# Row stages of a two-layer graph attention kernel: normalizing one tile per step, a third query buffer, transposed denominators, and last rows stored by tile

## The reference

```python
def _layernorm(x, axis=-1, eps=1e-5):
    m = jnp.mean(x, axis=axis, keepdims=True)
    v = jnp.var(x, axis=axis, keepdims=True)
    return (x - m) / jnp.sqrt(v + eps)
# layer 0
x_l = (x @ W + b).reshape(N, NHEADS, C)
scores = alpha_l[:, None, :] * alpha_r[None, :, :]      # alpha: x_l times att_l, att_r
att = softmax(where(adj[:, :, None] > 0, scores, NEG_INF), axis=1)
out = relu(einsum('ijh,jhc->ihc', att, x_l))
x = _layernorm(x + out)
# layer 1: queries are x, keys x2, values v, given as inputs
scores = where(adj > 0, einsum('hnd,hmd->hnm', q * C**-0.5, k), NEG_FILL)
x = _layernorm(x + einsum('hnm,hmd->hnd', softmax(scores), vv))
```

## Time and profile before

| | us |
|---|---|
| median of three runs | 3744.48 |
| the profiled execution, whole | 3745.04 |
| its span in the trace | 3743.1 |
| first row stage, from its first load to the first load of the next stage | 1674.07 to 1825.42 |
| second row stage, from the first load to the end of the span | 3640.46 to 3743.1 |
| TensorE busy over the span | 3551.1 (95%) |
| VectorE busy over the span | 2909.1 (78%) |
| ScalarE busy over the span | 2525.6 (67%) |

### The profile page before, as it was taken

The page is one execution under the profiler, slowest core; times in us unless marked ns, Lnnn a source line. Parts: engine busy times, 40 slices in busy tenths (PEclk is TensorE's granted clock), DMA queues, the critical chain, the costliest instruction groups (busy, mean ns, idle before and its releaser), DMA issues. The chain is left out here.

```text
span 3743.1 us, 58557 instructions
## 1 busy us (share of the span) xinstructions
PE 3551.1 (95%) x22661; PEld 1448.4 (39%) x22661; DVE 2909.1 (78%) x2948; ACT 2525.6 (67%) x2430; POOL 1569.5 (42%) x1157
## 2 busy tenths in 40 slices
PE   6888899999999999987699999999999999999987
PEld 4665222222222222225344444444444444444434
DVE  5555899999999999977577777777777777777768
ACT  3444899999999999963466666666666666666642
POOL 3333010010010101011267666767666677667661
PEclk9999899999999999995699999999999999999995
DMA  7887677677777776667699999999999999999987
GB/s 259 298 299 245 153 161 165 152 160 156 162 160 161 154 160 153 153 157 254 174 198 198 205 205 201 208 197 199 204 205 200 205 201 198 205 202 203 191 188 247
DMA packets 375357, 729.43 MB, mean 195 GB/s; under 512 B 31376, under 2 KB 219792, under 8 KB 358720
## 3 DMA queue, kind: packets, MB, share of 16 engines
q0 software_dynamic: 99504, 419.90, 57.7%
q1 hardware_dynamic: 241552, 272.26, 23.8%
q10 hardware_dynamic: 34048, 33.82, 2.7%
HBM read 263.54 MB, written 59.69 MB: 86 GB/s over the span
## 5 line engine op out<-in xcount | busy, mean ns | idle before, releaser
L1130 DVE TENSOR_TENSOR a_weights<-a_psS,maskT 128x1024 f32<-128x1024 f32 x1024 | 1205.5, 1219 | 463.5 <-ACT a_psS L1095 463.5
L1095 ACT ACTIVATE a_psS<-a_psS,a_shift 128x1024 f32<-128x1024 f32 x1024 | 1071.4, 1084 | 678.8 <-PE a_psS L1023 678.7
L538 DVE TENSOR_TENSOR g_weights<-g_weights,maskT 128x1024 f32<-128x1024 f32 x1024 | 1169.7, 1218 | 117.5 <-ACT g_weights L525 117.5
L525 ACT ACTIVATE g_weights<-al_bc,g_shift,g_xl 128x1024 f32<-128x1024 f32 x1024 | 1167.9, 1228 | 88.4 <-PE g_psD L563 88.4
L1023 PE MATMUL a_psS<-a_q,a_k 128*64 128x512 f16 x8192 | 971.6, 380 | 17.0 <-DMA a_k<-k_scratch 15.5
L1040 PE MATMUL a_psO<-a_weights,a_v 128*64 128x512 f32 x4096 | 961.2, 592 | 0.0
L554 PE MATMUL g_psO<-g_weights,g_xl 128*64 128x512 f32 x4096 | 924.1, 598 | 23.2 <-DVE g_weights L538 23.2
L1153 POOL TENSOR_TENSOR a_pool_total<-a_pool_total,a_weights 128x1024 f32<-128x1024 f32 x336 | 924.3, 2751 | 0.0
L1023 PEld LDWEIGHTS a_psS<-a_q,a_k 128*64 128x64 f16 x8192 | 463.4, 110 | 647.0 <-issue 300.4
L1161 POOL DMA_DIRECT2D a_dma_total<-a_weights x480 | 467.1, 973 | 399.6 <-DVE a_weights L1130 202.5
L554 PEld LDWEIGHTS g_psO<-g_weights,g_xl 128*64 128x64 f32 x4096 | 277.9, 137 | 660.5 <-issue 530.8
(11 more groups left out here) (121 smaller groups left out, 1451.0 us busy)
## 6 DMA issues: line engine op xcount, KB each, us to landing
a_dma_total<-a_weights POOLq DMA_DIRECT2D x512, 512.0 KB, 5.4
g_total<-g_weights POOLq DMA_DIRECT2D x128, 1024.0 KB, 7.7
adj_sb<-in_adj_dram SPq DMA_DIRECT2D x128, 512.0 KB, 5.9
g_xl<-xl_scratch SPq DMA_DIRECT2D x128, 260.0 KB, 6.7
a_k<-k_scratch SPq DMA_DIRECT2D x256, 128.0 KB, 5.4
a_v<-in_L_gnn_v_dram SPq DMA_DIRECT2D x128, 256.0 KB, 3.9
al_bc<-alpha_scratch SPq DMA_DIRECT2D x16, 1024.0 KB, 6.7
f_oT<-o_scratch SPq DMA_DIRECT2D x16, 1024.0 KB, 6.8
```

The source lines that it names most:

```text
L525: nc.scalar.activation(w[:, u % RING, h, :], al_bc[:, g % 2, h, :], ACT.Exp, bias=shift_bc[:, g % 2, h:h + 1], scale=xl[:, slot, u % KB, 2 ...
L538: nc.vector.tensor_tensor(w[:, u % RING, h, :], w[:, u % RING, h, :], maskT[:, j, (g // PAIRS) * IC:(g // PAIRS + 1) * IC], ALU.mult).then ...
L1095: nc.scalar.activation(psS[n % RING][:], psS[n % RING][:], ACT.Exp, bias=shift_bc[:, g % 2, h:h + 1], scale=SCALE).then_inc(exped, 1)
L1130: nc.vector.tensor_tensor(w[:, u % NP, h, :], psS[n % RING][:].rearrange("p a c -> p (a c)"), maskT[:, j, (g // PAIRS) * IC:(g // PAIRS + ...
```

## The change

- ScalarE normalizes tile t - 4 in step t, one tile per step, where it normalized four tiles in every fourth step. A group's store of 1 MB is issued behind its fourth tile, three steps later than before. The second row stage gets 36 steps where it had 33.
- The last group of either row stage is stored as four DMAs of 256 KB, each behind its own tile, where it was one of 1 MB.
- `qh` and `ql` have three buffers of a pair (QB = 3) where they had two, with three semaphores.
- The denominators are turned by a transpose (`is_transpose=True`) into `psR`, where they were a float32 matmul by the identity.

```diff
--- before.py
+++ after.py
@@ -624,6 +624,7 @@
         R = NT // T
         ZB = 3
         LAG = 7
+        QB = 3
         PARTS = (0, 32, 64)
         K = PARTS[-1] + H
         oT = sb("oT", [P, 2, PAIRS, T * P], F32)
@@ -665,8 +666,8 @@
         res_ready = sem("res_ready")
         res_stored = [sem(f"res_stored{i}") for i in range(ZB)]
         if first:
-            qh = sb("qh", [P, 2, PAIRS, 2 * P], F16)
-            ql = sb("ql", [P, 2, PAIRS, 2 * P], F16)
+            qh = sb("qh", [P, QB, PAIRS, 2 * P], F16)
+            ql = sb("ql", [P, QB, PAIRS, 2 * P], F16)
             v_sum = sb("v_sum", [P, F], F32)
             headmask = sb("headmask", [H, F], F32)
             next_sum = sb("next_sum", [H, F], F32)
@@ -675,11 +676,11 @@
             qh_ready = sem("qh_ready")
             ql_ready = sem("ql_ready")
             v_loaded = sem("v_loaded")
-            q_stored = [sem(f"q_stored{i}") for i in range(2)]
+            q_stored = [sem(f"q_stored{i}") for i in range(QB)]
             tail = sem("tail")
 
         block = ctx.enter_context(nc.Block())
-        STEPS = NT + LAG if first else NT + 1
+        STEPS = NT + LAG if first else NT + T
 
         @block.sync
         def _(sp):
@@ -724,9 +725,10 @@
                                  skip_group_check=True)
                 if t >= 2:
                     pe.wait_ge(inverted, t - 1)
-                nc.tensor.matmul(psR[t % 2][:], dT[0:H, par, cols], identF[0:H, 0:H], start=True, stop=False)
-                nc.tensor.matmul(psR[t % 2][:], alone[:, par, cols], times_n[:], start=False, stop=True
-                                 ).then_inc(turned, 1)
+                nc.tensor.matmul(psR[t % 2][:], dT[0:H, par, cols], identF[0:H, 0:H], is_transpose=True, start=True,
+                                 stop=False, skip_group_check=True)
+                nc.tensor.matmul(psR[t % 2][:], alone[:, par, cols], times_n[:], start=False, stop=True,
+                                 skip_group_check=True).then_inc(turned, 1)
 
             def turn_queries(t):
                 r, s = divmod(t, T)
@@ -756,35 +758,40 @@
                     act.wait_ge(rstd_ready, r - 1)
                 nc.scalar.activation(std[:, r % 2, :], mv[:, r % 2, :, 1], ACT.Sqrt, bias=eps[:]).then_inc(std_ready, 1)
 
-            def normalize(r):
-                act.wait_ge(rstd_ready, r + 1)
-                act.wait_ge(offset_ready, r + 1)
-                for s in range(T):
-                    nc.scalar.activation(z[:, r % ZB, s, :], z[:, r % ZB, s, :], ACT.Identity,
-                                         bias=offset[:, r % 2, s:s + 1], scale=rstd[:, r % 2, s:s + 1]
-                                         ).then_inc(res_ready, 1)
-                act.wait_ge(res_ready, T * (r + 1))
-                act.dma_start(result[r * T * P:(r + 1) * T * P, :].rearrange("(t p) c -> p t c", p=P),
-                              z[:, r % ZB, :, :]).then_inc(res_stored[r % ZB], 16)
+            def normalize(t):
+                r, s = divmod(t, T)
+                if s == 0:
+                    act.wait_ge(rstd_ready, r + 1)
+                    act.wait_ge(offset_ready, r + 1)
+                nc.scalar.activation(z[:, r % ZB, s, :], z[:, r % ZB, s, :], ACT.Identity,
+                                     bias=offset[:, r % 2, s:s + 1], scale=rstd[:, r % 2, s:s + 1]
+                                     ).then_inc(res_ready, 1)
+                if r == R - 1:
+                    act.wait_ge(res_ready, t + 1)
+                    act.dma_start(result[t * P:(t + 1) * P, :], z[:, r % ZB, s, :]).then_inc(res_stored[r % ZB], 16)
+                elif s == T - 1:
+                    act.wait_ge(res_ready, t + 1)
+                    act.dma_start(result[r * T * P:(r + 1) * T * P, :].rearrange("(t p) c -> p t c", p=P),
+                                  z[:, r % ZB, :, :]).then_inc(res_stored[r % ZB], 16)
 
             def upper(t):
                 pair, half = divmod(t, 2)
                 act.wait_ge(q_turned, t + 1)
-                if half == 0 and pair >= 2:
-                    act.wait_ge(q_stored[pair % 2], 32 * (pair // 2))
-                nc.scalar.activation(qh[:, pair % 2, :, half * P:(half + 1) * P], psQ[t % 3][:], ACT.Copy
+                if half == 0 and pair >= QB:
+                    act.wait_ge(q_stored[pair % QB], 32 * (pair // QB))
+                nc.scalar.activation(qh[:, pair % QB, :, half * P:(half + 1) * P], psQ[t % 3][:], ACT.Copy
                                      ).then_inc(qh_ready, 1)
 
             def store_queries(pair):
                 act.wait_ge(ql_ready, 2 * pair + 2)
                 for part, qq in enumerate((qh, ql)):
                     act.dma_start(q_dram[part].rearrange("(a p) n -> p a n", p=P)[:, :, pair * 2 * P:(pair + 1) * 2 * P],
-                                  qq[:, pair % 2, :, :]).then_inc(q_stored[pair % 2], 16)
+                                  qq[:, pair % QB, :, :]).then_inc(q_stored[pair % QB], 16)
 
             act.wait_ge(consts_set, 1)
             for t in range(STEPS):
-                if t > 0 and t % T == 0 and t <= NT:
-                    normalize(t // T - 1)
+                if T <= t < NT + T:
+                    normalize(t - T)
                 if t < NT and t % T == T - 1:
                     deviations(t // T)
                 if first and t >= LAG:
@@ -793,10 +800,10 @@
                         store_queries((t - LAG) // 2 - 1)
             if first:
                 store_queries(NT // 2 - 1)
-                for i in range(2):
-                    act.wait_ge(q_stored[i], 32 * (NT // 4))
+                for pair in range(NT // 2 - QB, NT // 2):
+                    act.wait_ge(q_stored[pair % QB], 32 * (pair // QB + 1))
             for r in range(R - ZB, R):
-                act.wait_ge(res_stored[r % ZB], 16 * (r // ZB + 1))
+                act.wait_ge(res_stored[r % ZB], 16 * (r // ZB + (T if r == R - 1 else 1)))
 
         @block.gpsimd
         def _(pool):
@@ -877,9 +884,9 @@
                 pair, half = divmod(t, 2)
                 cols = slice(half * P, (half + 1) * P)
                 dve.wait_ge(qh_ready, t + 1)
-                if half == 0 and pair >= 2:
-                    dve.wait_ge(q_stored[pair % 2], 32 * (pair // 2))
-                nc.vector.tensor_tensor(ql[:, pair % 2, :, cols], psQ[t % 3][:], qh[:, pair % 2, :, cols],
+                if half == 0 and pair >= QB:
+                    dve.wait_ge(q_stored[pair % QB], 32 * (pair // QB))
+                nc.vector.tensor_tensor(ql[:, pair % QB, :, cols], psQ[t % 3][:], qh[:, pair % QB, :, cols],
                                         ALU.subtract).then_inc(ql_ready, 1)
 
             for t in range(STEPS):
```

## The result

The changed kernel takes 0.9951 of the time before (95% interval 0.9938 to 0.9964): 3724.01 us median against 3742.98 in the same rounds. Measured again on another occasion, the ratio was 0.9951 (0.9938 to 0.9965). By the ratio, 0.0049 x 3744.48 = 18.3 us are gone; the forecast was 18.5. Runs of one kernel differ by up to 6 us (the kernel before: 3738.84 to 3744.8). Parts that no edit touches differ from trace to trace: in the thirteen traces of this study the first load of the first row stage starts between 1668.0 and 1674.1 us, and the attention of layer 1 lasts 1813.4 to 1816.1 us. A few us in a whole time can't be read, therefore. The lengths of the row stages, each from one profiled execution, can be read to about 1 us, and their repeating groups more closely (13.67 to 13.69 us in most).

What follows compares the result with a forecast made beforehand. VectorE was taken to set the first row stage's pace, idling mostly for ScalarE's rounding. 14.7 + 3.0 + 0.5 + 0.3 = 18.5 us off 3744.48 gave 3726.0 us, range 3722 to 3732.

Steps and rivals of the forecast that it cites:

- The stall at t % 4 = 0: First row stage: VectorE's subtraction waits for ScalarE's rounding behind four normalizations; 2.45 us, six times, 14.7 us to go.
- Behind the last tile: First row stage's end, bound by ScalarE's queue: last query store issued 2.97 us earlier; saving between 2.1 and 3.5.
- The recorded chain: ScalarE's queue after the first row stage's last offset, worked out instruction by instruction, with 0.92 us a query store.
- The third buffer: First row stage: frees roundings 28 and 30 of waits for query stores; in the steady part worth nothing.
- Denominators: Each row stage's first tile: one-pass transpose for two-pass product saves about 0.26 us, 0.5 in all; other tiles hidden.
- Last rows by tile: Kernel's end: last store issued 1.62 us later but lands sooner, 2.25 after issue; gain 0.3 us, bounds -0.5 and 0.7.
- Rival (a): First row stage becomes bound by DMA: at 291 GB/s 4.5 us come back, 3730.5, far end 3738.3; chance 0.15.
- (b): First row stage: the wait for the rounding persists, held by something other than the burst; 3740.7 us; chance 0.04.
- (c): Stage after the first row stage runs longer at the low clock, making the kernel slower, 3753.5 us; chance 0.02.

Runs made afterwards that it cites:

- The kernel with the moved rounding: Changed kernel with the queries' rounding put ahead of the square root at t % 4 = 3; 0.9938 of before, first row stage 126.85 us.

## Why the prediction was right, point by point

- **The size.** 18.5 us forecast, 18.3 by the ratio, 19.1 between the two traces. The ratio's interval means 13 to 23 us, so that it comes within 0.2 is more than the whole times can show. The stages can: 17.85 in the first row stage against 18.0 forecast there (14.7 + 3.0 + 0.26).
- **The stall at t % 4 = 0.** 14.7 forecast, 14.88 measured between steps 7 and 31. The rounding was ready 0.28 us early, where 0.17 was worked out.
- **Behind the last tile.** From the first last normalization to the last query store it was 14.74 us (1805.80 to 1820.54) and is 11.92 (1790.59 to 1802.51): 2.82 gone, 2.97 forecast. The recorded chain does not follow from the terms beside it: it gives its first two query stores 0.39 and 0.42 us where 0.92 is stated, without saying why. The trace bears the small values out, since a store's first issue runs beside the rounding ahead of it (1793.66 in a rounding from 1793.63 to 1794.23, the second issue done at 1794.66, 0.43 behind it).
- **The third buffer: the step that failed.** The prediction said that the removed waits are worth nothing in the steady part. That is true of the old order, as the run with three buffers alone shows. In the new one it is false: without the third buffer 3.0 us of the gain are missing in the six groups, beside what is missing behind them. The error was to judge a wait by the idle time it had before the change. With two buffers the `ql` store behind a square root (step 4k + 3) must land before the rounding of step 4k + 5, which takes 0.6 us, and the subtraction follows. From the store's issue to that subtraction it was 9.4 us before (1723.61 to 1732.99), with the stall of 2.45 us inside, and is 7.0 in the changed kernel (1720.62 to 1727.59): 8.8 and 6.3 us are left for the landing. These stores, in steps 11 to 23, landed 5.9 to 8.3 us after their issue before and 6.5 to 7.6 in the changed kernel with two buffers: no later, but now too late. The sum came out right because the change has both edits; for the steady part that was luck.
- **Tile by tile, or only the order.** The prediction removed the burst to get at the rounding behind it. The run with rounding ahead and three buffers shows that the order alone was the cause: with the burst kept, the stage is as short within 0.4 us. Normalizing by tile was one way to change the order. With two buffers it is the better way, by 2.6 us in the six groups (85.94 against 88.52).
- **Denominators.** 0.26 per row stage forecast; 0.32 in the wait of the first reciprocal (2.35 to 2.03), 0.33 against the product put back.
- **Last rows by tile.** 0.3 forecast, 0.65 measured. The mis-sized term was the landing: 2.0 us for 256 KB with only the store of the tile before still in flight, 2.25 worked out. The span ends 2.45 us behind the last issue, and 4.70 behind it before, so 2.25 are won there; the last issue comes 4.56 us behind the start of the last normalizations (3721.55 - 3716.99) against 2.96 before, 1.60 lost, so 0.65 is left. The fixed cost of some 2.0 us that the Trainium skill (DMA: Bandwidth & Descriptors, Anatomy of one DMA) gives would make the landing 2.6, an estimate worked out from it. That section describes DMAs that GpSimd issues; these are issued by ScalarE. The trace has 2.0 in all, and the measurement decides.
- **Rival (a), DMA.** Its traffic was right (305 to 312 GB/s and 0.97 to 1.00 in the windows, 310 and 1.01 worked out), its price not: 291 GB/s was taken as a limit from a stage that was not limited by DMA. The kernel with the moved rounding moves 326 GB/s without a wait of VectorE. Yet DMA did matter, by the landing of the stores that the third buffer absorbs.
- **Rivals (b) and (c).** No rounding stayed behind. The next stage starts at 0.58 of the clock in its first 16 us, 0.62 before, and it lasts 1815.13 us against 1815.04: no difference, where the stage varies by 2.7 us over thirteen traces.

The remaining 0.57 us of the second row stage's gain lies ahead of the last normalizations. 0.3 of it is the first tile's denominator; the rest is within what that stretch varies by from trace to trace (94.4 to 95.6 us over thirteen traces), and was not followed up.

## What to carry to other kernels

An engine with a fixed order of work makes others wait for whatever stands ahead of what they need: look for the instruction ahead of the needed one, and move the needed one first, before work is cut into pieces. When a stall is taken out, check each buffer again with the shorter period: a wait that was hidden in the stall may be the next bound, and two edits may be worth more together (17.4 us) than each alone (8.6 and 2.5). A busy share of DMA near 1 is not proof of a bound; ask whether an engine waits for a transfer, and for which one.

## What was not expected of the hardware

The DMA share of a window can exceed 1 (1.09 at 366 GB/s, over a whole group) while VectorE, ScalarE and TensorE there waited for no transfer, so 1.00 in this view is not a ceiling of the rate. And issuing a DMA is not of fixed length: a `ql` store of 256 KB held ScalarE's queue 0.53 us as a rule, 1.20 with a 1 MB store in flight, and up to 2.37 in the kernel that stores its queries twice (the row shown has 1.93, at 366 GB/s), and the ACTIVATE behind it waited.
